# A 3x3 convolution in five products per pair of output columns instead of six, in a three-stage fp32 kernel on Trainium2

## The reference, cut to what matters

```python
residual = x
h = jax.nn.relu(_bn_train(_conv(x, w1, 1, 0), g1, b1))   # 256 -> 64 channels, 1x1
h = jax.nn.relu(_bn_train(_conv(h, w2, 1, 1), g2, b2))   # 64 -> 64 channels, 3x3, one pixel of padding
h = _bn_train(_conv(h, w3, 1, 0), g3, b3)                # 64 -> 256 channels, 1x1
return jax.nn.relu(h + residual)
```

## Time and profile before

| What | us |
|---|---|
| Median of three runs | 856.8 |
| Span of the profiled execution, first to last instruction | 856.2 |
| TensorE busy in it | 800.9 |
| Layer 0, to the last matmuls of its last image | 0 to about 680 |
| From there to the first matmul of the second convolution | about 680 to 693.6 |
| The second convolution, first to last matmul | 693.6 to 763.9 |
| Second norm, third convolution's statistics | 763.9 to about 809 |
| Third convolution, add, store | about 809 to 856.2 |

### The profile page before, as it was taken

How to read it: one execution, slowest core, us unless ns; L and a number is a source line. 1 busy time by engine, 2 the same in 40 slices (tenths; PEclk the granted TensorE clock), 3 DMA queues, 4 the chain that set the end, 5 groups by cost and what they waited for, 6 DMA issues and landing times.

```text
span 856.2 us, 13886 instructions
## 1 busy us (share of the span) xinstructions
PE 800.9 (94%) x5016; PEld 731.5 (85%) x5016; DVE 653.7 (76%) x892; ACT 383.6 (45%) x661; POOL 335.2 (39%) x248
## 2 busy tenths in 40 slices
PE   6799988999999999999999999999986889996796
PEld 2259988999999999999999999999976777775685
DVE  4988898895888699688868968886484676129796
ACT  2542122444344344434434443442364787116397
POOL 4245664592485258238525823852200000006200
PEclk9999999999999999999999999999998989998999
DMA  9931218958984995899599587856399895020598
GB/s 271 384 111 35 50 29 220 239 149 228 179 226 115 245 205 143 224 178 231 120 241 212 136 225 149 211 126 185 88 263 274 242 325 235 1 94 5 190 427 364
DMA packets 250076, 162.17 MB, mean 189 GB/s; under 512 B 191849, under 2 KB 232794, under 8 KB 247194
## 3 DMA queue, kind: packets, MB, share of 16 engines
q1 hardware_dynamic: 241018, 141.31, 62.9%
q10 hardware_dynamic: 8992, 19.99, 7.1%
HBM read 99.48 MB, written 56.36 MB: 182 GB/s over the span
## 4 chain that ended last, share of the span: by engine, by line
PE 79%; DVE 11%; DMA 4%; issue 3%; ACT 2%; SPq 1%; POOL 1%; DVEq 0%; ACTq 0%
PE ps L1174 22%; PE ps L1176 22%; PE ps L1175 22%; PE ps L1294 4%; PE ps L1310 3%; PE ps L1344 3%; DVE y L2011 1%; DMA b2raw<-in_L_conv_b 1%; DMA xq<-in_x 1%; DVE wsum L1617 1%; DVE wpart L1617 1%; DVE hT L1576 1%; DMA x_dram<-x 1%; DVE whole L1667 1%; DMA raw<-bands 1%
## 5 line engine op out<-in xcount | busy, mean ns | idle before, releaser
L816 POOL TENSOR_TENSOR ring<-whole,ring 128x576 fp32r<-128x576 f32 x112 | 196.6, 1760 | 284.4 <-ACT ring L894 284.4
L1174 PE MATMUL ps<-w_hi,ring 128*128 128x336 f32 x832 | 275.9, 332 | 9.7 <-POOL ring L816 4.4
L1176 PE MATMUL ps<-w_hi,ring 128*128 128x336 f32 x832 | 263.1, 316 | 0.0
L1175 PE MATMUL ps<-w_lo,ring 128*128 128x336 f32 x832 | 261.9, 315 | 0.0
L1174 PEld LDWEIGHTS ps<-w_hi,ring 128*128 128x128 f32 x832 | 157.7, 190 | 19.9 <-issue 12.9
L1175 PEld LDWEIGHTS ps<-w_lo,ring 128*128 128x128 f32 x832 | 157.6, 189 | 0.0
L1176 PEld LDWEIGHTS ps<-w_hi,ring 128*128 128x128 f32 x832 | 156.8, 188 | 0.0
L894 ACT ACTIVATE ring<-whole 128x576 fp32r<-128x576 f32 x112 | 87.3, 784 | 89.9 <-POOL whole L811 46.5
L894 ACT ACTIVATE band_hi<-ps 128x320 fp32r<-128x320 f32 (+1 forms) x128 | 53.2, 419 | 131.7 <-PE ps L1294 124.2
L1174 PE MATMUL ps<-band_hi,xT_hi 128*128 128x224 f32 (+2 forms) x320 | 95.1, 297 | 0.6 <-DVE xT_lo L1576 0.3
L1175 PE MATMUL ps<-band_lo,xT_hi 128*128 128x224 f32 (+2 forms) x320 | 92.8, 290 | 0.0
(11 more groups left out here) (173 smaller groups left out, 1353.6 us busy)
## 6 DMA issues: line engine op xcount, KB each, us to landing
xq<-in_x SPq DMA_DIRECT2D x116, 256.0 KB, 4.9
raw<-bands SPq DMA_DIRECT2D x32, 768.0 KB, 7.0
xbuf<-in_x SPq DMA_DIRECT2D x16, 1024.0 KB, 9.4
x_dram<-x ACTq DMA_DIRECT2D x32, 512.0 KB, 5.8
x1in<-x_dram SPq DMA_DIRECT2D x7, 2048.0 KB, 12.9
bands<-wide SPq DMA_DIRECT2D x64, 199.0 KB, 4.9
out<-x1in SPq DMA_DIRECT2D x12, 1024.0 KB, 5.6
bands<-wide SPq DMA_DIRECT2D x3, 1792.0 KB, 15.7
```

What stands on the lines that cost most here:

```text
L816: pool.tensor_tensor(split(k, 1), positions(whole[:, k % TBUFS, :], 0, 2), split(k, 0).bitcast(F32), ALU.subtract).then_inc(sig_lo_done, 1)
L1174: pe.matmul(dst, l_hi, r_hi_, start=first, stop=False, **kw)
L1175: pe.matmul(dst, l_hi, r_lo_, start=False, stop=False, **kw)
L1176: return pe.matmul(dst, l_lo, r_hi_, start=False, stop=last, **kw)
```

## The change

For an image write e(c) and o(c) for its even and odd columns, and w0, w1, w2 for a filter's three columns. Before, an even output column was w0 o(c-1) + w1 e(c) + w2 o(c) and an odd one w0 e(c) + w1 o(c) + w2 e(c+1), six products. After, both share the product (w0 + w1) e(c). The even column adds w2 o(c) + w0 (o(c-1) - e(c)), the odd one w2 e(c+1) + w1 (o(c) - e(c)). The differences are called `left` and `step`.

- The weights `v2` get a fourth column, w0 + w1, made by two transposes into the same PSUM columns (15 transposes in place of nine). 
- The input of the stage lies in `yin`, [128, 8, 33, 32], where the shift of one row is in the layout, so that one copy serves both row parities. Its zero rows are set early. `y` now begins at the same address as `yin` and overwrites it, image by image.
- Four pairs of tiles take the place of `h1_hi` and `h1_lo`: `even` (rows of 34), `odd`, `left`, `step` (rows of 32, without gaps). Each holds two images, so that the pieces of image n wait for all products of image n - 2.
- TensorE computes for each image and half three banks: the shared product (6 matmuls), the even rest (12) and the odd rest (12). That is 240 matmuls.
- ScalarE copies the shared bank into `shared`; VectorE adds it to each of the other two, into `y`, and then takes the statistics.
- VectorE makes `left` and three low parts; GpSimd makes `step` and its low part.
- ScalarE waits for all of `y`'s stores before its first piece instead of before the last image; the wait for the last `x1_dram` store moves from VectorE and GpSimd to ScalarE, ahead of its first `step_hi`.

```diff
+        l1i = ExitStack()
+        yin = sb(l1i, "yin", [P, 8, SH + 1, SW])
+        shared = sb(l1i, "shared", [P, 2, HALF])
+        l1i.close()
+        l1y = ExitStack()
+        below = sb(l1y, "below", [P, 9, SPX])
+        y1_2 = sb(l1y, "y1_2", [MID1, 2, HALF])
+        l1y.close()
         y = sb(l1, "y", [P, 8, SPX])
+        hT = sb(l1, "hT", [P, 2, 4, 2 * P], F32R)
         v3_hi = sb(l1, "v3_hi", [P, 2, C], F32R)
...
-        h1_hi = sb(h1s, "h1_hi", [P, B, 2, SH + 1, SW + 2], F32R)
-        h1_lo = sb(h1s, "h1_lo", [P, B, 2, SH + 1, SW + 2], F32R)
+        even_hi = sb(h1s, "even_hi", [P, 2, SH + 1, SW + 2], F32R)
+        even_lo = sb(h1s, "even_lo", [P, 2, SH + 1, SW + 2], F32R)
+        odd_hi = sb(h1s, "odd_hi", [P, 2, SH + 1, SW], F32R)
+        odd_lo = sb(h1s, "odd_lo", [P, 2, SH + 1, SW], F32R)
+        left_hi = sb(h1s, "left_hi", [P, 2, SH + 1, SW], F32R)
+        left_lo = sb(h1s, "left_lo", [P, 2, SH + 1, SW], F32R)
+        step_hi = sb(h1s, "step_hi", [P, 2, SH + 1, SW], F32R)
+        step_lo = sb(h1s, "step_lo", [P, 2, SH + 1, SW], F32R)
...
-        v2_hi = sb(h1s, "v2_hi", [P, 6, P], F32R)
-        v2_lo = sb(h1s, "v2_lo", [P, 6, P], F32R)
+        v2_hi = sb(h1s, "v2_hi", [P, 8, P], F32R)
+        v2_lo = sb(h1s, "v2_lo", [P, 8, P], F32R)
+        left = sb(h1s, "left", [P, SH + 1, SW])
+        step = sb(h1s, "step", [P, SH + 1, SW])
...
-        PIECES = [(0, 0, HR + 1), (1, 0, HR + 1), (0, HR + 1, SH), (1, HR + 1, SH)] + [(i, 0, SH) for i in range(2, 8)]
...
+        PIECES = [(0, 0, HR + 1), (0, HR + 1, SH + 1)] + [(n, 0, SH + 1) for n in range(1, B)]
...
+        def relu_count(p, b):
+            return sum(4 if r1 - r0 > SH else 3 for n, r0, r1 in PIECES[0:p + 1]) - 1 + b
...
+        def piece_of(n, h):
+            return min(p for p, t in enumerate(PIECES) if t[0] == n and (h == 0 or t[2] == SH + 1))
...
+        def y_rows(g):
+            n, a, b = g // 4, (g // 2) % 2, g % 2
+            return yin[64 * a:64 * a + 64, 2 * n + b, a:a + SH, :].rearrange("m r c -> m (r c)")
...
+            return [(v[even, 0:4, even], 1), (v[even, 0:4, odd], 0), (v[even, 4:8, odd], 2),
+                    (v[odd, 0:4, even], 0), (v[odd, 4:8, even], 2), (v[odd, 4:8, odd], 1)]
...
-            sp.wait_ge(c2_done, 16)
+            sp.wait_ge(c2_done, 24)
             load_x1(5)
...
+            for t in (v3_hi, v3_lo):
                 pool.memset(t[:, :, :].bitcast(F32), 0.0).then_inc(corners, 1)
+            for a, r in ((0, SH), (1, 0)):
+                pool.wait_ge(corners, 2 + a)
+                pool.memset(yin[64 * a:64 * a + 64, :, r, :], 0.0).then_inc(corners, 1)
             pool.wait_ge(corners, 4)
+            pool.wait_ge(bt_done, NT * (STEPS - 1) + 5)
+            for t in (v2_hi, v2_lo):
+                pool.memset(t[:, :, :].bitcast(F32), 0.0).then_inc(corners, 1)
+            pool.wait_ge(corners, 6)
             pool.wait_ge(unit_done, len(UNITS) * STEPS)
             pool.wait_ge(y_done, 2 * STEPS)
...
-                    pool.wait_ge(x1_stored[1], 16 * STEPS)
-                    pool.wait_ge(y1_stored[1], 16 * STEPS // 2)
...
+            for t in (even_hi, even_lo):
+                pool.memset(t[:, :, :, SW:SW + 2].bitcast(F32), 0.0).then_inc(borders, 1)
             pool.wait_ge(vt_done, 2)
             pool.memset(cov[:, :], 0.0).then_inc(cov_zero, 1)
+            for p, (n, r0, r1) in enumerate(PIECES):
+                pool.wait_ge(relu1, relu_count(p, 1))
+                if p:
+                    pool.wait_ge(h1_hi_done, 4 * (p - 1) + STEP + 1)
+                    pool.wait_ge(step_lo_done, p)
+                pool.tensor_tensor(step[:, r0:r1, :], yin[:, 2 * n + 1, r0:r1, :], yin[:, 2 * n, r0:r1, :], ALU.subtract
+                                   ).then_inc(step_done, 1)
+                pool.wait_ge(h1_hi_done, 4 * p + STEP + 1)
+                pool.tensor_tensor(step_lo[:, n % 2, r0:r1, :], step[:, r0:r1, :], step_hi[:, n % 2, r0:r1, :].bitcast(F32),
+                                   ALU.subtract).then_inc(step_lo_done, 1)
             for i in range(8):
                 pool.wait_ge(centered, 2 * i + 2)
...
+            act.wait_ge(corners, 6)
             act.wait_ge(unit_done, len(UNITS) * STEPS)
...
+            def h1_part(p):
+                n, r0, r1 = PIECES[p]
+                if n >= 2:
+                    act.wait_ge(c2_done, 6 * (n - 1))
+                def main(b):
+                    part = yin[:, 2 * n + b, max(r0, 1):min(r1, SH), :]
+                    act.activation(part, part, ACT.Relu, bias=shift[:, 0:1], scale=scale[:, 0:1]).then_inc(relu1, 1)
+                def edge_row(a, r):
+                    rows = slice(64 * a, 64 * a + 64)
+                    part = yin[rows, 2 * n:2 * n + 2, r, :]
+                    act.activation(part, part, ACT.Relu, bias=shift[rows, 0:1], scale=scale[rows, 0:1]).then_inc(relu1, 1)
+                def high(dst, src):
+                    copy(dst, src).then_inc(h1_hi_done, 1)
+                if n == B - 1:
                     for h in range(2):
                         act.wait_ge(y1_stored[h], 16 * STEPS // 2)
...
+                if r0 == 0:
+                    edge_row(0, 0)
+                if r1 == SH + 1:
+                    edge_row(1, SH)
+                main(0)
+                if p:
+                    main(1)
+                act.wait_ge(relu1, relu_count(p, 0))
+                high(even_hi[:, n % 2, r0:r1, 0:SW], yin[:, 2 * n, r0:r1, :])
+                if not p:
+                    main(1)
+                act.wait_ge(relu1, relu_count(p, 1))
+                high(odd_hi[:, n % 2, r0:r1, :], yin[:, 2 * n + 1, r0:r1, :])
+                act.wait_ge(left_done, 2 * (p + 1))
+                high(left_hi[:, n % 2, r0:r1, :], left[:, r0:r1, :])
+                if not p:
+                    act.wait_ge(x1_stored[1], 16 * STEPS)
+                    act.wait_ge(y_done, 2 * STEPS)
+                act.wait_ge(step_done, p + 1)
+                high(step_hi[:, n % 2, r0:r1, :], step[:, r0:r1, :])
+            def c2_copy(j):
+                act.wait_ge(c2_done, 3 * j + 1)
+                if j >= 2:
+                    act.wait_ge(c2_sum, 2 * (j - 2) + 2)
+                copy(shared[:, j % 2, :], c2_bank(3 * j)).then_inc(c2_copied, 1)
+            for h in range(2):
+                act.wait_ge(y1_stored[h], 16 * STEPS // 2)
+            h1_part(0)
+            h1_part(1)
+            h1_part(2)
+            c2_copy(0)
+            c2_copy(1)
+            h1_part(3)
+            c2_copy(2)
+            c2_copy(3)
+            h1_part(4)
+            for j in range(4, 8):
+                c2_copy(j)
             def hT_hi(k):
                 act.wait_ge(hT_ps, k + 1)
                 if k >= 2:
...
+                    for ty in range(2 * k, 2 + k):
+                        at = (ty % 2) * 4 * MID1
+                        for t in range(3):
+                            pe.transpose(psR[k][:, at + t * MID1:at + (t + 1) * MID1], v2raw[0:MID1, :, 3 * ty + t::9],
+                                         ident[0:MID1, 0:MID1])
+                        for t in range(2):
+                            mm = pe.matmul(psR[k][:, at + 3 * MID1:at + 4 * MID1], v2raw[0:MID1, :, 3 * ty + t::9],
+                                           ident[0:MID1, 0:MID1], start=t == 0, stop=True, is_transpose=True, skip_group_check=t == 1)
                     if k == 1:
                         for cb in range(CB):
                             mm = pe.transpose(psR[1][:, C + cb * P:C + (cb + 1) * P], v3raw[:, cb, :, :], ident[:, :])
...
             pe.wait_ge(vT_done, 2)
-            pe.wait_ge(borders, 8)
...
-                taps = sorted(range(6), key=lambda t: (b + t % 3 - 1) % 2)
...
+            pe.wait_ge(borders, 2)
+            def c2_product(n, h, which, q):
+                if q >= 8:
+                    j, r = divmod(q - 8, 3)
+                    if r == 0:
+                        pe.wait_ge(c2_copied, j + 1)
+                    else:
+                        pe.wait_ge(c2_sum, 2 * j + r)
+                p = piece_of(n, h)
+                for i, (made, hi, lo, f, col) in enumerate(which):
+                    pe.wait_ge(made, p + 1)
+                    for s in range(2):
+                        rows = slice(HR * h + s, HR * h + s + HR)
+                        mm = mm3(c2_bank(q), v2_hi[:, 4 * s + f, :], v2_lo[:, 4 * s + f, :],
+                                 hi[:, n % 2, rows, col:col + SW], lo[:, n % 2, rows, col:col + SW],
+                                 (i, s) == (0, 0), (i, s) == (len(which) - 1, 1))
                 mm.then_inc(c2_done, 1)
+            for j in range(8):
+                n, h = divmod(j, 2)
+                c2_product(n, h, [(even_lo_done, even_hi, even_lo, 3, 0)], 3 * j)
+                c2_product(n, h, [(odd_lo_done, odd_hi, odd_lo, 2, 0), (left_lo_done, left_hi, left_lo, 0, 0)], 3 * j + 1)
```

(57 more changed lines are left out.)

74 lines of the change are left out of this document (14 added, 60 removed).

## The result

The changed kernel takes 847.8 us, median of four runs (846.8 to 848.7), against 857.4 for the kernel before in its four. The ratio is 0.9871, 95% interval 0.9852 to 0.9890. The profiled execution has a span of 845.4 us and took 847.3.

The account below looks back on a forecast made before the run. TensorE's matmuls were taken to bound the second convolution (busy 70.00 of 70.00 us). From 856.8 us, start +0.55, matmuls -13.1, stalls +3.2 and end +0.1 gave -9.2: 847.6 us, range 844.6 to 851.5.

Parts of the forecast that it names:

- Removed matmuls and layout: Second convolution: 48 fewer matmuls save 11.7 us, 144 reading adjacent pixels save 1.5; 57.0 us instead of 70.1.
- layout worth nothing: Rival: second convolution's matmul spacing stays 0.2435 us throughout, 1.5 us of gain lost; 848.7 us, chance 0.17.
- The start: Ahead of the second convolution: weights and moved store wait put the first matmul at 694.15, 0.55 us later.
- the 5.8 us for the store to land: Last `y` store, issued at 684.54, was to land 5.8 us later, at 690.3, ahead of ScalarE's first piece.
- The lower bound of the range, 844.6: Low end of the forecast range: no exclusion between VectorE and GpSimd, and the `y` store lands 0.8 us sooner.
- The stalls: TensorE waits at the first piece (1.3 us) and image 1 (0.65 and 1.25), 3.2 us together; bounds 0 and 5.
- Exclusion: VectorE's two-tile and GpSimd's subtractions follow one another, from a 3.68 us GpSimd subtraction, normally 1.43; stalls 3.2 us, otherwise 1.0.
- no exclusion: Rival: VectorE and GpSimd run side by side, or stalls are hidden otherwise; 1.0 us instead of 3.2, 845.4, chance 0.15.
- The pieces' pace: Making an image's pieces takes 13.1 us, against 14.2 for TensorE's 60 matmuls, so covered on average.
- the ring of two: Tiles hold two images, so image 2 waits for image 0's products; no stall claimed at images 2 and 3.
- the rival at 868: Rival: making the pieces sets the pace, 21.3 us an image, 7.1 over TensorE's, three times; 868 us, chance 0.04.
- The end: Last bank: a sum of 0.684 us and one wait replace a copy of 0.604 ahead of the statistics; 0.1 us more.

Follow-up runs that it names:

- e2: Changed kernel with the shared product computed twice, once per column parity, so 288 matmuls again; ratio to the kernel before 0.9979, stage 69.02 us.
- e1: Changed kernel with both parts of `step` kept in rows of 34, like `even`; stage 59.66 us against 58.56.
- e7: Changed kernel with one idle matmul instead of 14 ahead of the stage; stage 59.02 us, 61.76 from the first ReLU.
- e10: Changed kernel with `step` and `step_lo` on VectorE, next piece's ReLUs earlier, `y` store wait later, 12 idle matmuls for 14; ratio to the kernel before 0.9851.
- e11: Changed kernel run again without an edit; ratio to the kernel before 0.9882, median 848.1 us, stage 59.04 us.
- e3: Changed kernel with the one-column operation of `left` moved from VectorE to ScalarE; stage 58.04 us against 58.56.
- e5: Changed kernel with GpSimd's first `step` waiting until VectorE has made the first `odd_lo`; stage 60.06 us against 58.56.
- e6: Changed kernel with `step` and `step_lo` made by VectorE, none by GpSimd; stage 56.96 us against 58.56.

## Why the prediction was right, point by point

**How near, and how much of that was luck.** The forecast was 847.6 us and the median is 847.8; the medians fell by 9.6 us for 9.2. The mechanism is what the prediction said. But the sum was made against the profiled span, and that fell by 10.8 us, so the steps were off by 1.6 us together; that the median came out 0.2 from the forecast is in part luck with the executions that were profiled.

**Removed matmuls and layout.** Predicted 57.0 us for 240, measured 56.8 (56.5 for the 239 spacings), as `odd`, `left` and `step` came to 0.232 rather than 0.2333. e2 gives the 48 matmuls back and with them all but 0.2% of the gain; e1 turns the layout's 0.011 us a matmul on and off for one tile. The rival "layout worth nothing" is refuted.

**The start.** Predicted 694.15, measured 693.84. The chain to the last `y` store came 1.33 us later, but 0.49 of that was there before the transposes (680.73 against 680.24): chance from one execution to the other. The fifteen transposes take 1.86 us for nine's 1.17, 0.69 where I had 0.78. The step that failed is the 5.8 us for the store to land: it took 4.66 us here and 4.7 to 5.2 in the other runs. So the moved wait cost 0 to 0.6 us and not always the 0.6 of the sum. (The lower bound of the range, 844.6, has a slip of its own: it lets the store land 0.8 us sooner, but by the prediction's sum the scale comes only 0.6 us ahead of it, and would then hold ScalarE up.) And `even_lo` was there at 693.23, but the first matmul came 0.61 us later. In e7, e10 and e11 the same hand-over takes 0.14, so some 0.5 us went on the idle matmuls, which no step had:

```profile
688.18 5.91 PE L1569 MATMUL ps<-ident 128*128 128x128 f32 x28
```

It cost nothing in the end, for the seventh matmul waited for `odd_lo` all the same (61.76 us from the first ReLU, 61.78 in e11).

**The stalls: the mis-sized term.** Predicted 3.2 us, measured 2.0, in e11 2.4. The places were the right ones: behind the sixth matmul (1.3 predicted, 0.5 measured) and image 1's first and second bank (0.65 and 1.25 predicted; 0.3 and 0.8 measured), none later. At the first piece the difference is mostly the start: TensorE was held by the idle matmuls for 0.5 us and so waited less for `odd_lo`; in e11, where it wasn't, it waited 0.9. At image 1 it is ScalarE's list. I had added 0.05 us between its operations; they overlap:

```profile
705.21 1.07 ACT L923 ACTIVATE even_hi<-yin 128x1056 fp32r<-128x1056 f32 x1
706.19 1.06 ACT L923 ACTIVATE odd_hi<-yin 128x1056 fp32r<-128x1056 f32 x1
```

The second begins 0.09 us before the first ends. Some nine such places before image 1, at 0.14 us each (the 0.09 and my 0.05), make 1.3 us by estimate; `even_hi` of image 1 ended 15.64 us after ScalarE's start (706.28 - 690.64), where I had 16.9. Against that worked GpSimd's `step` of 1056 elements, 2.47 us where I had 1.9. The Trainium skill has this number: ScalarE: Activation LUTs, section "What ACT_TABLE_LOAD costs", says that back-to-back ACTIVATEs overlap by about 93 ns. The trace agrees where the two operations are independent, and the number was there to be used in the sum; a copy that needs the ReLU before it begins 0.03 us after its end (691.82 for 690.99 + 0.80).

**Exclusion.** The 3.68 of the earlier trace rows carried over to other shapes: 1.34 us for 17 elements, 2.66 for `even_lo` in the changed kernel; e3 moves the hold from the column to `odd_lo`; e5 removes it at one place; e6 takes GpSimd out and all subtractions have their own length. The rival "no exclusion", whose 845.4 had a chance of 0.15, is refuted. The Trainium skill's SBUF — State Buffer, section "SBUF: two separate sides", gives the rule (an exclusive lock on a shared pair of ports between GpSimd and a VectorE operation with two SBUF inputs, held for a whole instruction), with which these rows agree. The column operation has one SBUF input, for which the rule wants a two-port mode; it was held, and no run here shows in which mode it worked.

**The pieces' pace.** No gap at images 2 and 3, in any run (no spacing over 0.28 us): the ring of two is long enough, and the rival at 868 has nothing for it.

**The end.** 0.1 predicted, 0.09 measured. What follows the aggregation took 0.2 us more, in which no step had a part. In sum the span fell by 10.8 us where the steps gave 9.2: 0.3 more from the start, 1.2 from the stalls, 0.3 from the spacing (69.89 - 56.5 = 13.4 for 13.1), less 0.2 behind the stage.

**The expectations that failed.** e7's (59.5 to 61) lay above what was measured, for it left out that a slow engine waits less; e3's, for ScalarE's list, which the column operation had held up; e5's, for a queue behind a waiting instruction (`step_hi`) that I hadn't followed; e6's, for counting VectorE's busy time where the shared access was the queue.

## What to carry to other kernels

Cut TensorE's work where a window shows it busy without a pause at the full clock, and count spacings, not durations: here 48 x 0.2435 us gave nearly the whole gain. If VectorE and GpSimd have two-input operations on SBUF in the same stretch, as here, add their durations into one list; an operation moved from GpSimd to VectorE can shorten that list (1.25 us for 2.47) though it makes the busier engine busier. Write each engine's queue out in order before moving a step: in e5 what hurt was not the moved instruction, but what stood behind the one that waited for it. And measure a stage from the event that releases it, here the first ReLU: that number repeated within 0.03 us, where the stage's own length varied by 0.5.
